# The second feed-forward in two halves that overlap across turns

## The reference, cut to what matters

```python
H, P, G, NS, K = (8, 64, 64, 64, 3)
...
fx = (x @ W_fx.T + b_fx).reshape(B, N, H, P).transpose(0, 2, 1, 3)
xm = (x @ W_x.T + b_x).reshape(B, N, H, P).transpose(0, 2, 1, 3)
sw = jax.nn.softmax((xm @ W_slice.T + b_slice) / temp, axis=-1)
snorm = sw.sum(2)
st = jnp.einsum('bhnc,bhng->bhgc', fx, sw) / (snorm + 1e-05)[..., None]
...
ot = _hydra(st, ...)   # z, x, B, C, dt; taps over tokens; softplus(dt); scan both ways; gate; norm
...
out = jnp.einsum('bhgc,bhng->bhnc', ot, sw).transpose(0, 2, 1, 3).reshape(B, N, D_INNER)
return out @ out_w.T + out_b
```

## Time and profile before

| what | us |
|---|---|
| device time, median of 3 runs | 3499.8 (3492.73 to 3500.13) |
| span of the profiled execution, first to last instruction | 3243.7 |
| TensorE busy in the span | 2606.3 (80%) |
| VectorE busy | 2274.7 (70%) |
| ScalarE busy | 1783.4 (55%) |
| GpSimd busy | 867.6 (27%) |

### The profile page before, as it was taken

How to read it: one execution, slowest core, us unless ns; L and a number is a source line. 1 busy time by engine, 2 the same in 40 slices (tenths; PEclk the granted TensorE clock), 3 DMA queues, 4 the chain that set the end, 5 groups by cost and what they waited for, 6 DMA issues and landing times. The chain is left out here.

```text
span 3243.7 us, 68706 instructions
## 1 busy us (share of the span) xinstructions
PE 2606.3 (80%) x19386; PEld 2087.8 (64%) x19386; DVE 2274.7 (70%) x6679; ACT 1783.4 (55%) x5130; POOL 867.6 (27%) x863
## 2 busy tenths in 40 slices
PE   5899996992776941789999999699996888759992
PEld 4577776992675941656776777566664555549992
DVE  6777774666685656667777777499997688835555
ACT  2344434663674532755565555377774777726664
POOL 0233334663343432300000000000001155534442
PEclk9899997996887975989999999799998999969996
DMA  5111112334321213200000000000001000012225
GB/s 200 46 59 59 59 34 76 84 84 127 125 77 48 66 59 118 82 1 1 0 0 0 0 0 1 22 21 21 24 19 67 5 28 28 29 42 65 63 62 175
DMA packets 142548, 168.55 MB, mean 52 GB/s; under 512 B 19920, under 2 KB 118224, under 8 KB 141776
## 3 DMA queue, kind: packets, MB, share of 16 engines
q1 hardware_dynamic: 116688, 118.67, 12.1%
q0 software_dynamic: 21504, 44.74, 4.0%
q10 hardware_dynamic: 4224, 3.59, 0.4%
HBM read 115.87 MB, written 51.05 MB: 51 GB/s over the span
## 5 line engine op out<-in xcount | busy, mean ns | idle before, releaser
L1198 POOL DMA_INDIRECT y_rows<-ffn_e_rows_out,ffn_e_scatter_at x352 | 339.7, 965 | 385.7 <-DVE ffn_e_rows_out L1226 218.4
L1340 PE MATMUL bank<-ffn_e_xT,ffn_e_mine 128*128 128x128 f32 x3360 | 439.6, 278 | 2.2 <-ACT ffn_e_xT L1272 1.4
L1340 PEld LDWEIGHTS bank<-ffn_e_xT,ffn_e_mine 128*128 128x128 f32 x3360 | 410.4, 195 | 3.4 <-ACT ffn_e_xT L1272 2.2
L722 POOL DMA_INDIRECT sorted_rows<-ffn_rows,ffn_slot x320 | 315.5, 986 | 278.8 <-issue 266.4
L1274 ACT ACTIVATE ffn_e_mine<-constants 128x512 f32 (+1 forms) x352 | 250.2, 712 | 114.6 <-issue 65.3
L1246 DVE TENSOR_TENSOR ffn_e_hid<-ffn_e_act,bank 128x256 f32<-128x256 f32 (+1 forms) x280 | 136.1, 486 | 225.0 <-ACT ffn_e_act L1300 199.8
L1350 PE MATMUL bank<-ffn_e_mine,ffn_e_hid 128*128 128x128 f32 x1968 | 278.0, 276 | 2.6 <-DVE ffn_e_hid L1250 2.4
L2566 ACT ACTIVATE gnn_prob<-bank,gnn_low 128x256 f32<-128x256 f32 x512 | 203.5, 501 | 107.1 <-DVE gnn_low L2480 107.1
L1350 PEld LDWEIGHTS bank<-ffn_e_mine,ffn_e_hid 128*128 128x128 f32 x1968 | 247.5, 192 | 5.3 <-DVE ffn_e_hid L1250 4.8
L1300 ACT ACTIVATE ffn_e_act<-bank 128x256 f32<-128x256 f32 (+1 forms) x280 | 120.9, 432 | 106.0 <-PE bank L1340 104.9
L2480 DVE TENSOR_REDUCE gnn_low<-bank 128x2 f32<-128x512 f32 x256 | 159.0, 684 | 24.1 <-PE bank L2665 21.3
(11 more groups left out here) (505 smaller groups left out, 6583.6 us busy)
## 6 DMA issues: line engine op xcount, KB each, us to landing
g_adj<-in_adjT SPq DMA_DIRECT2D x48, 512.0 KB, 4.0
ffn_e_rows_in<-sorted_rows SPq DMA_DIRECT2D x346, 66.0 KB
ffn_c_y<-y_rows SPq DMA_DIRECT2D x80, 256.0 KB, 3.2
g_adj_rows<-in_adj SPq DMA_DIRECT2D x16, 512.0 KB, 4.3
gnn_adj<-in_adjT SPq DMA_DIRECT2D x16, 512.0 KB, 4.0
constants<-in_ffn SPq DMA_DIRECT2D x1, 6281.0 KB, 22.2
y_rows<-ffn_e_rows_out,ffn_e_scatter_at POOLq DMA_INDIRECT x352, 2.2
constants<-in_ffn SPq DMA_DIRECT2D x1, 5204.0 KB, 15.4
```

Of the source, the lines that this page charges most:

```text
L722: eng.indirect_dma_start(c.sorted_rows, bass.IndirectOffsetOnAxis(r.slot[par][:, k, j:j + 1], 0), r.rows[par][:, j, :], None).then_inc(r.d ...
L1198: g.indirect_dma_start(c.y_rows, bass.IndirectOffsetOnAxis(scatter_at[par][:, k:k + 1], 0), rows_out[par][:, k, :], None).then_inc(scatter ...
L1340: ins = pe.matmul(chunk(part, ch), chunk(weights[:, i * HALF:(i + 1) * HALF], ch), x, start=True, stop=True)
```

## The change

The feed-forward is cut in two halves. Pooling, projections, convolution and dt of turn t (the front) are issued beside running sums, decay, y, gate, norm and the tail of turn t - 1 (the back); the fins and the residual are those of turn t - 2. The sums over `ones` go: half of the columns of each stationary `value_w` block are ones, so that the same 8 products give numerators and denominators, on the two halves of the partitions. The scan matrices are compacted: since the graphs are independent, each has 64 instead of 128 columns for a head, and G and y are products of 64 x 64 blocks, two for each matrix. The spreading of dt (`dt_run`, both directions, and `dt_both`) is three GpSimd instructions of 128 x 512 instead of eight on ScalarE and two on VectorE. sz and swT have two buffers; the banks are dealt out anew.

```diff
-                def pool_sums(t, g):
...
+                def pool_values(t):
+
+                    pe.wait_ge(ph_ready, t * 2 + 2)
+                    wait_past(pe, xpad_ready, t)
+                    for a in range(2):
+                        for j in range(KC):
+                            cols = slice((2 * j + a) * SL, (2 * j + a + 1) * SL)
+                            ins = mm(B[5 - a][:, j * P:(j + 1) * P], value_w[:, a, j, :], pooled_h[:, :, cols], start=True, stop=True)
                     ins.then_inc(st_ps, 1)
...
+                def spread_dt(t, first):
+                    g.wait_ge(dt_ready, t + 1)
...
+                    for d in range(2):
+                        ins = g.tensor_tensor(dt_run[:, d], per_head(dt[:, d * HEADS2:(d + 1) * HEADS2], SL),
+                                              own_masks[:, d, None, :].broadcast_to([P, HEADS2, SL]), ALU.mult)
...
+                    g.tensor_tensor(dt_both[:], dt_run[:, 0], dt_run[:, 1], ALU.add).then_inc(dt_both_ready, 1)
```

GpSimd's new turn is `skip_term(t - 1)`, the addition of `out_b` to X, `norm_power(t - 1)`, `spread_dt(t)`. VectorE's new turn, in order (here and below `back` is every turn but the first, `settled` every turn but the first two):

```diff
+                    if back:
+                        scan_factor(t - 1)
+                    if more:
+                        soft_a(t + 1, 0)
+                    pooled(t)
+                    if more:
+                        soft_b(t + 1, 1 - par, 0)
+                    if back:
+                        scan_decay(t - 1)
+                    if more:
+                        soft_a(t + 1, 1)
+                    v.wait_ge(tz_ready, t + 1)
+                    v.scalar_tensor_tensor(sz[par][:], tz[:], 1.0, B[6][:], ALU.add, ALU.mult).then_inc(sz_ready, 1)
+                    if back:
+                        gated(t - 1, 1 - par)
+                    if more:
+                        soft_b(t + 1, 1 - par, 1)
+                    v.wait_ge(xpad_ready, t + 1)
+                    then(v, tap_last(xpad, conv_x, w["convb_x"], xc, range(KC)), conv, t * 4 + 1)
+                    then(v, tap_more(1, xpad, conv_x, xc, range(KC)), conv, t * 4 + 2)
+                    v.wait_ge(bcd_ready, t + 1)
+                    then(v, v.tensor_tensor(u[:], dtr[:], w["dt_bias"], ALU.add), sp, t * 13 + 1)
+                    v.scalar_tensor_tensor(m[:], u[:], -1.0, u[:], ALU.mult, ALU.min).then_inc(spm_ready, 1)
+                    if back:
+                        mean_of_squares(t - 1)
+                    if more:
+                        soft_a(t + 1, 2)
+                    tap_more(0, xpad, conv_x, xc, range(KC)).then_inc(xc_ready, 1)
+                    if settled:
+                        residual(t - 2)
...
+                    if back:
+                        normed(t - 1)
+                    if more:
+                        soft_b(t + 1, 1 - par, 2)
+                    time_step(t)
+                    if more:
+                        soft_a(t + 1, 3)
```

```diff
+                    wait_past(pe, bcd_ready, t)
+                    pool_h(t, par, 0)
+                    if more:
+                        to_features(t + 1, 1 - par)
+                    wait_past(pe, sz_ready, t)
+                    pool_h(t, par, 1)
+                    if back:
+                        tokens_T(t - 1)
+                    if settled:
+                        fin_piece(t - 2, par, 0)
+                    if back:
+                        product_G(t - 1)
+                    pool_values(t)
+                    if more:
+                        lg_piece(t + 1, 0)
+                    if back:
+                        running_sums(t - 1)
+                    swT_piece(t, par, 0, last)
+                    if settled:
+                        fin_piece(t - 2, par, 1)
+                    swT_piece(t, par, 1, last)
+                    if settled:
+                        fin_piece(t - 2, par, 2)
+                    swT_piece(t, par, 2, last)
+                    project_z(t)
+                    if back:
+                        decay_seen(t - 1)
+                    if more:
+                        lg_piece(t + 1, 1)
+                    if back:
+                        product_y(t - 1)
+                    project_x(t)
+                    project_bcd(t)
+                    if more:
+                        lg_piece(t + 1, 2)
+                    if settled:
+                        fin_piece(t - 2, par, 3)
+                    swT_piece(t, par, 3, last)
+                    if back:
+                        tail_y(t - 1)
                     if more:
                         lg_piece(t + 1, 3)
...
+                    if back:
+                        tail_o(t - 1)
+                        tail_p(t - 1, False)
```

More of the change, by code:

```diff
@@ new lines, in mean_of_squares, with normed, turn @@
+                def mean_of_squares(t):
+                    v.wait_ge(ms_ready, t + 1)
+                    v.tensor_scalar(ve[:], ms[:], 1.0 / IN2, 1e-5, ALU.mult, ALU.add).then_inc(ve_ready, 1)
+                def normed(t):
+                    v.wait_ge(rstd_ready, t + 1)
+                    v.scalar_tensor_tensor(yn[:], yg[:], rstd[:], w["norm_w"], ALU.mult, ALU.mult).then_inc(yn_ready, 1)
+                def turn(t, par, first, last):
+                    more, back = not last, not first
+                    settled = back and not (isinstance(t, int) and t == 1)
+                    if first:
+                        all_but_last(1, h[1]).then_inc(h_ready, 1)
+                    if back:
[28 more added lines that the diff above has]
+                        residual(t - 2)
+                    then(v, tap_last(bcpad, conv_bc, w["convb_bc"], bc, range(1)), conv, t * 4 + 3)
+                    then(v, tap_more(1, bcpad, conv_bc, bc, range(1)), conv, t * 4 + 4)
+                    tap_more(0, bcpad, conv_bc, bc, range(1)).then_inc(bc_ready, 1)
+                    if back:
[5 more added lines that the diff above has]
+                        soft_a(t + 1, 3)
@@ new lines, in product_y, with turn @@
+                def product_y(t):
+                    for g in range(2):
+                        rows_ = slice(g * SL, (g + 1) * SL)
+                        for hd in range(HEADS2):
+                            cols = slice(hd * HD2, (hd + 1) * HD2)
+                            ins = mm(B[7][rows_, cols], decay[rows_, hd, :], xtok[rows_, cols], start=True, stop=True)
+                    ins.then_inc(y_ps, 1)
+                def turn(t, par, first, last):
+                    more, back = not last, not first
+                    settled = back and not (isinstance(t, int) and t == 1)
+                    wait_past(pe, bcd_ready, t)
[13 more added lines that the diff above has]
+                        lg_piece(t + 1, 0)
+                    if back:
+                        running_sums(t - 1)
[7 more added lines that the diff above has]
+                    project_z(t)
+                    if back:
+                        decay_seen(t - 1)
+                    if more:
+                        lg_piece(t + 1, 1)
+                    if back:
+                        product_y(t - 1)
+                    project_x(t)
+                    project_bcd(t)
@@ L2347, in turn @@
                     if more:
                         lg_piece(t + 1, 2)
-                    if not first:
-                        tail_p(t - 1, more)
+                    if settled:
+                        fin_piece(t - 2, par, 3)
+                    swT_piece(t, par, 3, last)
+                    if back:
+                        tail_y(t - 1)
                     if more:
                         lg_piece(t + 1, 3)
-                    if not first:
-                        fin_piece(t - 1, 0)
@@ L2355, in turn @@
-                    swT_piece(t, par, 0, None if more else 1)
-                    if not first:
-                        fin_piece(t - 1, 1)
-                    swT_piece(t, par, 1)
-                    if not first:
-                        fin_piece(t - 1, 2)
-                    pe.wait_ge(xT_ready, t + 1)
-                    for k in range(KC):
-                        ins = pe.transpose(B[5][:, k * P:(k + 1) * P], xT[:, k, :], c.ident[:])
-                    ins.then_inc(xt_ps, 1)
-                    pe.wait_ge(bct_ready, t + 1)
@@ L2374, in turn @@
-                    pe.wait_ge(dt_back_ready, t + 1)
-                    for half in range(2):
-                        for d in range(2):
-                            ins = mm(B[6 + half][:], masks[:, 1 - d, :], dt_run[d][:, half * 4:half * 4 + 4, :].rearrange("p a n -> p (a n)"),
-                                     start=(d == 0), stop=(d == 1))
-                        ins.then_inc(D_ps, 1)
-                    swT_piece(t, par, 2)
-                    if not first:
-                        fin_piece(t - 1, 3)
@@ L2404 @@
+                tail_o(end)
+                tail_p(end, True)
+                for k in range(TT):
+                    fin_piece(end, 1, k)
 HD_G, HD_A = 16, 32
```

344 lines of the change are left out of this document (158 added, 186 removed).

## The result

The changed kernel takes 3599.2 us (median of 4 runs, 3597.2 to 3604.8) against 3500.0 for the kernel before (4 runs): ratio 1.0291, interval 1.0276 to 1.0307. It is slower by 99 us; the forecast was 3576.

What follows compares the result with a forecast made beforehand. TensorE was taken to set the pace at 41.6 us a turn; 13 full steps x 4.4 = 57, ends 2 and clock 18 make 77 us on the median of 3499.8: forecast 3576 us, range 3525 to 3635.

Steps and rivals of the forecast that it cites:

- TensorE's work: TensorE's own instructions in one turn: 34.9 us after the change, 3.1 us less than before.
- Wait B: TensorE idle at `tail_y(t-1)` for `yn`: a chain of 8.7 us from X against 4.0 of work, 4.7 us.
- Wait C: TensorE idle at `tail_p(t-1)` for otT's copy, behind `exp_piece(t+1, 3)`: 8.2 us against 4.9 of work, 3.3 us.
- TensorE alone: Stretch from `tail_p` through lg 0 in which TensorE works without waiting: 11.2 us a turn.
- Wait A: TensorE idle at the second `swT_piece` for ScalarE's first copy: 6.1 us against 3.1 of work, 3.0 us.
- X: The end of `project_x` in a turn; the stretch of TensorE work leading back to it was put at 11.8 us.
- The turn: One steady turn: 46.0 us, of which 11.1 waits, against 41.6 before; 4.4 us more, the clock apart.
- the ends: First turns and drain of the feed-forward, counted together at +2 us, an estimate within 8.
- The clock: Falls to half clock following waits: 0.7 of a fall a turn on the path, 1.3 us, 18 us in all.
- The 256 us "outside the span": Median of 3499.8 us less the profiled span of 3243.7, taken as time outside the span that does not change.
- Rival 3: TensorE stays the bound, early `normed` and `soft_a` 3 removing Waits B and C: 38.0 us a turn, 3455 us; chance 0.09.
- GpSimd at nothing: GpSimd's three dt matrix instructions, 3 x 1.04 us, cost nothing, even if they block VectorE's two-input instructions throughout.

Runs made afterwards that it cites:

- e7: e6 with `all_but_last(t + 2)` (`f_h`) moved on VectorE from the turn's end to behind `soft_b` 0; 3459.8 us, ratio 0.988.
- e9: The changed kernel with `product_y`'s loops exchanged, so that the two 64 by 64 tiles alternate; 3558.3 us (one run).
- e2: The changed kernel with `tail_o` ahead of `exp_piece` 3 on ScalarE alone; 3598.7 us, ratio 1.0294.
- e6: The changed kernel with e4's order and the back half moved up on VectorE, ScalarE and TensorE, to shorten all three waits; 3245.3 us, ratio 0.9995.
- e10: e8 with e9's exchanged `product_y` loops; 3186.5 us, ratio 0.9816.
- e4: The changed kernel with decays and two `swT` copies ahead of `exp_piece` 0 on ScalarE, `pooled` and `scan_decay` earlier on VectorE; 3294.4 us, ratio 1.0147.
- e5: The changed kernel with four unused 512-column products put ahead of the second `swT_piece` in each turn; 3562.1 us, ratio 1.0186.
- e1: The changed kernel with `normed(t - 1)` moved on VectorE to right behind the last x tap; 3573.8 us, ratio 1.0226.
- e3: e1 with the copies of otT and of `tail_p` ahead of `exp_piece` 3 on ScalarE; 3348.1 us, ratio 1.0313.
- e0: The kernel before, run again unchanged for a second trace; 3498.6 us (one run).
- a1: The changed kernel, run again unchanged; 3600.5 us, ratio 1.0289.
- e8: e7 with the dt matrix moved from GpSimd back to VectorE, behind `soft_b` 3; 3456.2 us, ratio 0.9875.

## Why the prediction was right, point by point

**Forecast and result.** 3576 in a range of 3525 to 3635, slower at 0.86; measured 3599. The mechanism, three waits and a lower clock, is what the trace shows, and e7 shows that it is the order and not the work: with two of the waits cut to 1 us or less and B gone the same operations take 38.1 us a turn.

**TensorE's work.** Forecast 34.9 us; e7, without slow stretches, has 35.3. y was forecast at 2.1 and takes 1.83; G's eight small ones at 0.67 and take 0.37 from start to start. On the page of the Trainium skill that I weighed there (TensorEngine Tiling (Array Packing), Key Properties): that different tiles run in parallel holds here once they alternate (e9, 1.07 us, the "near 1 us" of the forecast). In the order of the change, eight heads of one tile in a row, there is none of it: 0.057 us each, half the price of an instruction with 128 columns.

**Wait B.** Forecast 4.7 from a chain of 8.7; measured 4.71 (4.36 to 4.96 over the turns) and 8.85.

**Wait C.** Forecast 3.3, measured 1.28. Two terms were off and nearly cancelled. `exp_piece` 3 is done sooner than I had it, and TensorE's three groups, `tail_y`, lg 3 and `tail_o`, take 7.6 us for 4.9 because the clock falls after B; the copy then waits for `tail_o` alone (e2). From `tail_y` to `tail_p` it is 8.90 us, forecast 8.2, and that the two lie so close is luck. The forecast that wait C takes up the fall after B was thus only partly true: it took up 2.0 us of the fall, from 3.3 down to 1.28, and 0.7 us stand on the path.

**TensorE alone.** Forecast 11.2, measured 11.1.

**Wait A.** Forecast 3.0, measured 2.38 (the decays 1.76 rather than 1.9, and the chain 5.59 rather than 6.1). The stretch behind it to X, 13.36 us for 11.8, holds the fall: 1.6 us on the three groups behind A (0.79, 1.71 and 0.85 us from start to start).

**The turn.** 8.85 + 8.90 + 11.1 + 5.59 + 13.36 = 47.8; forecast 46.0 and 1.3 for the clock, 47.3. Thirteen steps give +80 for 75.

**The term that was mis-sized: the ends.** Forecast +2 within 8. From the stage's start to the first `f_term` 88.5 us for 73.2, from the last on 40.4 for 34.2, and the two steps at the rims as long as two of before: +21. Together 80 + 21 = 101, the measured 101.4. The first turns and the drain have little beside them, and chains that are covered in a steady turn stand there in full, with a low clock behind most. The longest is one that I had put at nothing: `f_h`, made at the end of VectorE's turn, keeps TensorE for 9.73 us in turn 1. `f_h` alone isn't the cause, though: in e7, which makes it early, TensorE waits 6.21 us for the last piece of `f_sw` at the same place, and the head is as long as e6's (85.4 and 85.0 us). In the drain the new wait is the decay, 2.61 us. I had looked at what work the ends lose and gain, not at their chains. How far another order mends it can be read from e7 and e10: the stage less its thirteen steady steps is 190 us before, 212 after, 198 in e7 and 190 in e10.

**The clock.** Forecast 0.7 of a fall a turn on the path, 1.3 us. After A it falls in every turn, 1.6 us, and 0.7 more come from behind B; removing wait A gives more than its idle time, and only filling it gives 2.3 us a turn (e4, e5). The rule of the Trainium skill (TensorE: Matmul & The Clock Gate, Why this matters for your kernels) that long idle gaps bring the low rate agrees with B's rows in the kernel after (4.4 to 5.0 us, each followed by a fall), and not with the 3.25 us in the earlier trace rows. For shorter waits the length alone doesn't tell: 2.38 us at A were followed by a fall in every steady turn of the kernel after and, past the first turns, by none in e9, and the waits of 2.52 and 1.1 to 1.5 us at `tail_y` and `tail_o` by one in every other turn of e1 and in nearly every turn of e3. Why isn't settled.

**The 256 us "outside the span".** That reading was wrong, though it did no harm: nothing like that lies outside (3597.2 against a span of 3595.3). It is the difference between two kinds of chips.

**The rivals.** Rival 3 (TensorE stays the bound: 38.0 us a turn) is not what the change does, but it is what e7 reaches, 38.1, by the route that the rival named: `normed` and `soft_a` 3 early enough. That the numbers meet is partly luck, for the rival kept wait A at 3.0 us and had B and C at nothing, and e7 has waits of 1.00, 0.85 and 0.99. It also took something that the rival did not name: `f_h`, which is next once B is gone (e6, 2.58 us). GpSimd at nothing holds for a steady turn of the kernel after, where TensorE does not wait for `f_h`; in e6 it does, and the 2.5 us that GpSimd adds there are read from the rows, not tested alone.

**Open.** Which part of the ends' 21 us is idle time and which is the clock. The changed kernel wasn't run on the chips where before takes 3247 us. How the head's 15 us divide over its chains; moving `f_h` alone did not shorten it. None of the compaction's parts was tried alone in the old order.

## What to carry to other kernels

When two stages are overlapped, add up for each engine's queue what stands ahead of the instruction that the pacing engine waits for, from its last hand-over on; less work on the pacing engine wins nothing if a chain in the new order is longer than the work left to cover it. Shorten all such chains together, in the order in which they would come due: here B and C, taken out one after the other, passed most of their time to the next (e1, e3), and all of them together, with `f_h`, turned +101 us into -38 (e7). On TensorE an idle stretch can cost nearly as much again in the slower work behind it (here 2.4 us idle and 1.6 us slow at A), and at the ends of a loop, where little stands beside them, count each chain in full.

## What the runs showed of the hardware

- Float32, tiles of 64 by 64, 64 columns: 32 instructions on two tiles in turn take 1.07 us (e9); one tile's sixteen, then the other's, 1.83 (after).
- Four unused products of 512 columns in a wait of each turn made the stage 30 us shorter (e5), by the clock alone.
- The same waits need not bring the same fall of the clock: in e1 A is 2.38 us and B 2.52 in every turn, and the fall comes behind A in one turn and behind B in the next (`tail_o` 3.84 us, then 6.1 to 6.2).
- VectorE beside GpSimd, both on data in SBUF: `scalar_tensor_tensor` of 64x128 takes 1.13 us instead of 0.28, and GpSimd's two products 2.47. The Trainium skill (SBUF — State Buffer, Who interferes with whom) says that a VectorE instruction with two SBUF inputs and a GpSimd one that reads SBUF exclude each other for a whole instruction; Bt's time agrees: it starts 0.43 us after the first of the two GpSimd products (half of 2.47 us each) and ends 0.3 us behind that product's end, which is its own 0.28.
- The same kernel takes 3499 us on two chips (e0, e1, e2, e5; a1, e7, e8, e9) and 3247 and 3246 on two others (e3, e4, e6; e10), 7%, with none of it in the stage studied here.
